# First dense attention: eviction of projections and turned sums on ACT, rotary products on POOL

## The chip, the cores and the metric

One core of one Trainium2 chip. The metric is the device time of the whole program in microseconds (us); lower is better. The program is a chain of eight layers' parts; the change touches only the first dense attention.

## The reference, cut to what matters

```python
def _L0_attn_ref(x, qkv_w, qkv_b, out_w, out_b):      # x: 4 x 1024 x 128, 16 heads of 8
    qkv = x @ qkv_w + qkv_b
    q, k, v = jnp.split(qkv, 3, axis=-1)
    ...
    q = apply_rotary(q)      # x1*cos - x2*sin, x2*cos + x1*sin
    k = apply_rotary(k)
    scores = jnp.einsum('bhqd,bhkd->bhqk', q, k) * SCALE
    weights = jax.nn.softmax(scores, axis=-1)
    attn = jnp.einsum('bhqk,bhkd->bhqd', weights, v)
    return attn.transpose(0, 2, 1, 3).reshape(B, T, D) @ out_w + out_b
```

## The kernel before, in words

The attention handles 4 batches of 8 pairs of heads, 32 pairs `p` in all, and each pair has 8 steps `k` of 128 keys. One generator, `order()`, writes down the work; every engine walks through the same list and picks its own items, so each engine's queue is in that order.

A step: PE makes four score blocks (L460, 128x512, three PSUM banks in turn: 4, 5 and 7), between them four blocks of scores for the row maxima of pair p+2 (L452, banks 0 to 3), and then the weighted sums of the step before (L534). ACT takes the exponential of each score block (L585), which frees its bank. DVE takes two row maxima (L640). Once in a pair come `parts` (four small DVE operations, L703 to L709, at step 0), `send` (step 1: a PE transpose, a DVE copy L716, and on SP a store L860 and, when it has landed, two loads L867, which bring the maxima to the operands of a later pair; a pair's first score waits for them) and `divide` (step 3).

`spread()` puts the preparation of the next batch into pairs 1 to 3 of each of the first three batches, always behind a step: eight `qk` items, a projection of 512 columns each (PE L468, two instructions), for query and key, for either half `hf`, and for x = 0 (the weights) and x = 1 (the weights with the columns of a turn swapped). They stand at steps 2, 5 and 7. Their PSUM bank is one of the three of the scores. DVE evicts them (L668): (product + bias) times cosine or sine, into `QF` and `R1`. After each x = 1 comes a `split` on POOL: the sum QF + R1 (L797), then four operations (L802 to L805) that split it into three bfloat16 parts, and SP stores these (L836). `QF` and `R1` are one set, so a `qk` waits until the `split` before has ended. The last `split` of a batch comes at step 5 of pair 3 of the batch (p = 3, 11, 19).

`fetch` (SP, L854, 24 DMAs of 64 KB) loads the operands of the next four pairs from these stores. For the next batch it stands at step 0 of pairs 4, 12 and 20, and waits for the stores of the last `split`. SP's queue is in order: the `send` of the following pair (its L860 and L867) stands behind it. The same holds of the `send` at step 1 of pair 3, which stands behind the stores of the third `split`.

POOL also gathers and adds the rows of the mixture of experts in pairs 1 to 9 (`row` items, L1131, L1140, L1143, four in a pair), in the same in-order queue as the splits.

At pairs 8, 16 and 24, steps 4 to 7, stand `turn` and `proj` of the batch before, twice each: a transposition of the attention's output on PE (L550), its eviction by DVE (L750), the output projection on PE (L557), and on DVE the addition to the residual (L759) and four statistics (L884). Those of the last batch end the stage.

Of the kernel before, what the change touches and what calls it, by code (L numbers as in the profile page):

```python
# [15 lines left out]
NB = 4  # L16
# [128 lines left out]
def program(nc, a, out):  # L145
    ctx = ExitStack()
    with ctx:
# [22 lines left out]
        def bank(key):  # L170
            return core.banks.of[key]
# [104 lines left out]
        def attention(first, wq, wk, wv, bq, bk, bvb, wo, extra, load, row, mix=None):  # L276
# [4 lines left out]
            with ExitStack() as c:  # L281
# [9 lines left out]
                part = [[sb([128, 512], BF16, c) for _ in range(3)] for _ in range(2)]  # L291
                QF = sb([128, 512], F32, c)
                R1 = sb([128, 512], F32, c)
                P = [sb([128, 4 if first else 8, 512], F32, c) for _ in range(4)]
                OS = sb([128, 512], F32, c)
                ATT = sb([128, 8, 128], F32, c)
# [143 lines left out]
                def pe(e):  # L440
# [22 lines left out]
                    for what, *i in order():  # L463
                        if what == "qk":
                            b, qi, hf, x = i
                            bm = early.next() if b == 0 else ring.next()
                            take(e, bm, (what, *i), (DV, (what, *i)))
                            e.op.matmul(PS[:, bm, :], W[qi][x], XT[:, b * T + hf * 512:b * T + hf * 512 + 512],  # L468
                                        start=True, stop=True).then_inc(*PM.up((what, *i)))
                        elif what == "v":  # L470
# [30 lines left out]
                        elif what == "tile":  # L501
                            p, ps, blk, ti = i
                            u0, nu = TILES[ti]
                            bk = 3 * (n % 2)
                            n += 1
                            if fills(p, 4 * ps + blk, ti):
                                bm = take(e, ring.next(), ("fill", *i))
                                e.op.matmul(PS[:, bm, 0:384], ident[:], XT[:, 0:384], start=True, stop=True)  # L508
                            take(e, bk, (what, *i), (AC if ps else PW, (what, *i)))
                            rows_in(e, p)  # L510
                            if gated(p, ps):
                                e.wait_ge(ONES, "ones")
                            for x in range(nu):
                                y = u0 + x
                                t = score(bk + x, p, 2 * blk + y // 4, y % 2, y // 2 % 2,
                                          KG if gated(p, ps) else KS)
                            t.then_inc(*SC.up((what, *i)))
                            SC.at["unit", p // 4] = SC.n
                        elif what == "pv":
                            p, kb = i  # L520
                            e.wait_ge(DV, ("v", p // 8, 1))
                            e.wait_ge(DV, "zeroed")
                            if first:
                                e.wait_ge(PW, (p, kb, 1, 1))
                            else:
                                e.wait_ge(DG, (p, kb // 2, 1 + kb % 2))
                            if kb == 0:
                                take(e, PVB, ("pv", p), (AC if first else DV, ("os", p)))
                            for side in range(2):
                                for hf in range(2):  # L530
                                    gq = 32 * (2 * side + hf)
                                    x = 2 * hf + side
                                    src = P[(8 * p + kb) % 4][:, x, :] if first else P[kb // 2][:, 4 * (kb % 2) + x, :]
                                    t = e.op.matmul(PS[gq:gq + 9, PVB, :], Vx[p // 8 % 2][:, kb, 8 * side + p % 8, :],  # L534
                                                    src, start=kb == 0, stop=kb == 7)
                            t.then_inc(*PV.up((p, kb)))
                        elif what == "divide":
                            p, = i
                            bm = take(e, ring.next(), ("divide", p), (DV, ("att", p)))
                            e.wait_ge(AC if first else DV, ("os", p))  # L540
                            for k in range(4):
                                t = e.op.transpose(PS[:, bm, k * 128:(k + 1) * 128], OS[:, k * 128:(k + 1) * 128],  # L542
                                                   ident[:])
                            t.then_inc(*PM.up(("divide", p)))
                        elif what == "turn":
                            b, j = i
                            bm = take(e, (ends if b == NB - 1 else ring).next(), ("turn", b, j), (DV, ("turn", b, j)))
                            e.wait_ge(DV, ("att", 8 * b + 7))
                            for k in range(4):
                                t = e.op.transpose(PS[:, bm, k * 128:(k + 1) * 128], ATT[:, 4 * j + k, :], ident[:])  # L550
                            t.then_inc(*PM.up(("turn", b, j)))
                        elif what == "proj":
                            b, j = i
                            bm = take(e, (ends if b == NB - 1 else ring).next(), ("proj", b, j), (DV, ("proj", b, j)))
                            e.wait_ge(DV, ("turn", b, j))
                            for k in range(4):
                                t = e.op.matmul(PS[:, bm, k * 128:(k + 1) * 128], ATT_T[j][:, 128 * k:128 * k + 128],  # L557
                                                wo, start=True, stop=True)
                            t.then_inc(*PM.up(("proj", b, j)))

                def act(e):
                    n = 0
                    loaded(e)
                    for what, *i in order():
# [9 lines left out]
                            e.op.copy(first_parts[qi][hf][1][:], QS[hf][:]).then_inc(*AC.up(("middle", qi, hf)))  # L574
                        elif what == "fetch" and i[0] == 0:
                            fetch_first(e, 1)
                        elif what == "step":
                            p, k = i
                            x = 8 * p + k
# [34 lines left out]
                def dve(e):  # L614
# [28 lines left out]
                    for what, *i in order():  # L643
                        if what == "qk":
                            b, qi, hf, x = i
                            bb = BB[qi][x]
                            e.wait_ge(PM, (what, *i))
                            if b == 0:
                                if qi:
                                    e.wait_ge(PO, ("split", 0, 0, hf))  # L650
                                src = PS[:, bank((what, *i)), :]
# [8 lines left out]
                                else:  # L660
# [1 line left out]
                                        *DV.up((what, *i)))  # L662
                                    DV.at["sum", qi, hf] = DV.n
                                continue
                            e.wait_ge(PO, ("split", b, qi, hf - 1) if hf else
                                      ("split", b, 0, 1) if qi else ("split", b - 1, 1, 1))
                            if first:
                                e.op.scalar_tensor_tensor(  # L668
                                    out=(QF, R1)[x][:], in0=PS[:, bank((what, *i)), :], scalar=bb,
                                    in1=extra[x][:, hf * 512:hf * 512 + 512], op0=ALU.add, op1=ALU.mult).then_inc(  # L670
                                    *DV.up((what, *i)))
                            else:
                                e.op.tensor_scalar(QF[:], PS[:, bank((what, *i)), :], bb, None, ALU.add).then_inc(  # L673
                                    *DV.up((what, *i)))
                        elif what == "split" and i[0] == 0:
# [54 lines left out]
                        elif what == "divide":  # L730
# [7 lines left out]
                            for side in range(2):  # L738
# [3 lines left out]
                                    view[:, side, :, :, 0:8],  # L742
                                    rc[:, side].unsqueeze(3).broadcast_to([128, 2, 4, 8]), ALU.mult).then_inc(
                                    *DV.up(("att", p)))
                        elif what == "turn":
                            b, j = i
                            e.wait_ge(PM, ("turn", b, j))
                            if b:
# [15 lines left out]
                def pool(e):  # L764
# [11 lines left out]
                    for what, *i in order():  # L776
# [9 lines left out]
                        elif what == "split":  # L786
                            b, qi, hf = i
                            pt = part[hf]
                            if b == 0:
                                e.wait_ge(AC, ("middle", qi, hf))  # L790
                                pt = first_parts[qi][hf]
                                e.op.tensor_tensor(pt[2][:], QS[hf][:], pt[1][:], ALU.subtract).then_inc(
                                    *PO.up(("split", b, qi, hf)))
                                continue
                            e.wait_ge(DV, ("qk", b, qi, hf, NX - 1))
                            if first:
                                then().tensor_tensor(QF[:], QF[:], R1[:], ALU.add).then_inc(*PO.up())  # L797
                            if qi:
                                e.wait_ge(SENT[hf], (b, 0, hf))
                            else:  # L800
                                e.wait_ge(SENT[hf], (b - 1, 1, hf))
                            then().tensor_copy(pt[0][:], QF[:]).then_inc(*PO.up())  # L802
                            then().tensor_tensor(QF[:], QF[:], pt[0][:], ALU.subtract).then_inc(*PO.up())
                            then().tensor_copy(pt[1][:], QF[:]).then_inc(*PO.up())
                            then().tensor_tensor(pt[2][:], QF[:], pt[1][:], ALU.subtract).then_inc(  # L805
                                *PO.up(("split", b, qi, hf)))

                def sp(e):
# [2323 lines left out]
```

## Time and profile before

| | |
|---|---|
| median of 3 runs | 4427.58 us (4419.74 to 4429.66) |
| the profiled execution | 4435.13 us, span 4433.3 us |
| PE, DVE, ACT, POOL busy, of the span | 76%, 62%, 57%, 31% |
| L640, row maxima, DVE | x512, 601.0 us busy, 1216 ns each |
| L585, exponentials, ACT | x1024, 532.4 us busy, 603 ns each |
| L460, scores of both attentions, PE | x3072, 738.6 us busy |

Busy time is the time in which an engine executes; the engines work side by side, so the shares do not add up. The stage of the change lies between 489 and 1231 us of the span.

### The profile page before, as it was taken

The page shows a single profiled execution, that of the slowest core. Times are in us where ns is not written, and L with a number is a line of the kernel's source. Part 1 is how long each engine was busy: PE and PEld are TensorE (multiplying, and loading weights), DVE is VectorE, ACT ScalarE, POOL GpSimd, SP SyncE. Part 2 cuts the span into 40 slices and gives each one's busy share as a digit, 9 for nine tenths or more (in the row PEclk, how much of TensorE's full clock was granted, in tenths as well). Part 3 has the DMA queues.
Part 4 walks back from the last instruction along what each step waited for, and adds up shares of the span by engine and source line. Part 5 has one row for each costly group of instructions (what it writes and reads, how often), then busy time and mean ns, then how long its engine had stood idle before and what let it go on. Part 6 is the DMA issues. An engine that isn't in the chain of part 4 may idle for free. (4 is left out here: it accounts for less than half of the span.)

```text
span 4433.3 us, 53632 instructions
## 1 busy us (share of the span) xinstructions
PE 3348.3 (76%) x20118; PEld 1505.0 (34%) x20182; DVE 2764.3 (62%) x4523; ACT 2540.8 (57%) x4189; POOL 1356.0 (31%) x1221
## 2 busy tenths in 40 slices
PE   7597788889948888988887887889868697541126
PEld 4265122212211222222222565466544274211124
DVE  5123889989736556655655776477667121488886
ACT  2112477767858989999995776377533222212225
POOL 0401283010012010010001885388411403218880
PEclk9698799999979999999997999899889798775558
DMA  4002121210020010010100111011020021550000
GB/s 136 33 22 57 29 48 32 33 31 16 2 47 17 14 27 17 15 23 7 15 1 29 28 35 36 14 34 35 17 81 8 30 60 33 73 66 0 10 5 24
DMA packets 140025, 137.36 MB, mean 31 GB/s; under 512 B 42184, under 2 KB 104692, under 8 KB 139764
## 3 DMA queue, kind: packets, MB, share of 16 engines
q1 hardware_dynamic: 130612, 116.07, 12.4%
q0 software_dynamic: 8192, 16.79, 1.6%
q8 instruction: 159, 2.61, 0.2%
q10 hardware_dynamic: 960, 1.05, 0.1%
q14 instruction: 102, 0.84, 0.1%
HBM read 64.90 MB, written 33.82 MB: 22 GB/s over the span
## 5 line engine op out<-in xcount | busy, mean ns | idle before, releaser
L460 PE MATMUL PS<-t 50*128 50x512 bf16 (+2 forms) x3072 | 738.6, 397 | 203.4 <-ACT t L603 53.8
L585 ACT ACTIVATE t<-PS 128x512 f32<-128x512 f32 x1024 | 532.4, 603 | 239.3 <-PE PS L460 233.9
L722 DVE TENSOR_TENSOR t<-t 128x1536 f32<-128x1536 f32 (+1 forms) x384 | 583.5, 1587 | 131.3 <-ACT t L603 77.8
L640 DVE TENSOR_REDUCE t<-PS 128x1 f32<-128x1024 f32 x512 | 601.0, 1216 | 54.0 <-PE PS L452 50.0
L534 PE MATMUL PS<-t 128*9 128x512 f32 x4096 | 551.1, 611 | 9.9 <-DVE t L722 9.5
L605 ACT ACTIVATE t<-PS 128x1536 f32<-128x1536 f32 (+1 forms) x384 | 477.7, 1311 | 53.7 <-PE PS L460 38.4
L603 ACT ACTIVATE t<-PS 128x1536 f32<-128x1536 f32 (+1 forms) x384 | 476.9, 1311 | 35.9 <-PE PS L460 20.9
L460 PEld LDWEIGHTS PS<-t 50*128 50x128 bf16 (+2 forms) x3072 | 158.4, 94 | 985.6 <-ACT t L603 276.2
L452 PE MATMUL PS<-t 48*128 48x512 bf16 x1024 | 342.0, 404 | 46.8 <-DVE t L640 24.0
L1798 POOL TENSOR_TENSOR t<-t 128x512 f32<-128x512 f32 x128 | 159.8, 1270 | 589.5 <-DVE t L1473 476.0
L2613 PE MATMUL PS<-t 128*128 128x32 f32 x256 | 61.1, 403 | 344.7 <-ACT t L2659 280.9
L508 PE MATMUL PS<-t 128*128 128x384 f32 x544 | 268.9, 579 | 1.6 <-DVE t L673 1.6
L1122 POOL DMA_INDIRECT scr<-t x128 | 126.3, 987 | 270.6 <-DVE t L1115 232.2
L2677 ACT COPY t<-PS 128x640 f32<-128x640 f32 x64 | 44.3, 692 | 277.0 <-DVE PS L2779 272.4
L1131 POOL DMA_INDIRECT t<-scr,t x128 | 123.6, 966 | 254.7 <-DMA scr<-t 181.9
L802 POOL CAST t<-t 128x512 bf16<-128x512 f32 x24 | 24.8, 1034 | 575.8 <-DVE t L673 574.2
L734 DVE RECIPROCAL t<-PS 128x16 f32<-128x16 f32 x64 | 16.5, 258 | 279.8 <-PE PS L542 277.0
L1685 ACT ACTIVATE t<-PS,t 128x128 f32<-128x128 f32 x512 | 179.9, 381 | 2.3 <-DVE t L1759 1.9
L2613 PEld LDWEIGHTS PS<-t 128*128 128x128 f32 x256 | 56.9, 328 | 350.2 <-ACT t L2659 285.6
L2177 PE MATMUL PS<-t 128*128 128x512 f32 x256 | 131.7, 665 | 26.8 <-issue 21.1
L2693 POOL TENSOR_TENSOR t<-t 128x256 f32<-128x256 f32 x124 | 104.4, 842 | 148.6 <-ACT t L2677 141.3
L1214 PE MATMUL PS<-t 128*128 128x320 f32 x512 | 149.6, 452 | 0.0
(403 smaller groups left out, 6380.0 us busy)
## 6 DMA issues: line engine op xcount, KB each, us to landing
t<-scr SPq DMA_DIRECT2D x336, 64.0 KB
t<-t SPq DMA_DIRECT2D x128, 128.0 KB, 2.3
scr<-t SPq DMA_DIRECT2D x96, 128.0 KB
t<-t SPq DMA_DIRECT2D x16, 512.0 KB, 13.3
scr<-t SPq DMA_DIRECT2D x2, 2560.0 KB
t<-scr SPq DMA_DIRECT2D x16, 320.0 KB, 3.6
scr<-t SPq DMA_DIRECT2D x16, 320.0 KB, 2.6
t<-scr SPq DMA_DIRECT2D x48, 48.0 KB
```

What stands on the lines that cost most here:

```text
L452: t = e.op.matmul(PS[:, 2 * side + hf, :], Qx[p // 4 % 2][lo:lo + KP, j, qc * 128:qc * 128 + 128], Kx[p // 4 % 2][lo:lo + KP, j, hf * 512: ...
L460: return e.op.matmul(PS[:, bk, :], Kx[p // 4 % 2][lo:lo + rows, j, kb * 128:kb * 128 + 128], Qx[p // 4 % 2][lo:lo + rows, j, hf * 512:hf * ...
L508: e.op.matmul(PS[:, bm, 0:384], ident[:], XT[:, 0:384], start=True, stop=True)
L534: t = e.op.matmul(PS[gq:gq + 9, PVB, :], Vx[p // 8 % 2][:, kb, 8 * side + p % 8, :], src, start=kb == 0, stop=kb == 7)
L585: e.op.activation(P[x % 4][:, 2 * hf + side, :], PS[:, bank((what, p, k, side, hf)), :], ACT.Exp, scale=S8).then_inc(*PW.up((p, k, side, hf)))
L603: t = e.op.activation(dst, PS[:, bk:bk + nu, :], ACT.Sigmoid, scale=S8)
L605: t = e.op.activation(dst, PS[:, bk:bk + nu, :], ACT.Exp, scale=S8)
L640: e.op.tensor_reduce(MX[p % 2][:, side, qc:qc + 1], PS[:, 2 * side:2 * side + 2, :].rearrange("p a n -> p (a n)"), AX, ALU.max).then_inc(* ...
L722: e.op.tensor_tensor(o, o, SGM[(12 * p + 3 * blk + ti) % 3][:, 0:nu, :], ALU.mult).then_inc(*DG.up((p, blk, ti)))
L1214: t = e.op.matmul(PS[:, b + hf, 0:320], ws[x % slots][i][:, f * 128:(f + 1) * 128], XE[x % 2][:, 320 * hf:320 * hf + 320], start=True, sto ...
L1685: e.op.activation(PB[i][:, h, :], PS[:, SB + h % 2, 128 * (h // 2):128 * (h // 2) + 128], ACT.Exp, bias=mx[i][:, h:h + 1], accum_out=su[i] ...
L1798: e.op.tensor_tensor(sn[:, :, :, lo:lo + 32], x[:, :, :, 32 - lo:64 - lo], TS[:, n % 8, :, lo:lo + 32].unsqueeze(2).broadcast_to([128, 2, ...
```

## The change

The projections of batches 1 to 3 are evicted by ACT, with the bias added and no factor; POOL multiplies both halves by cosine and sine ahead of the sum. `QF` and `R1` have a second set, one for each half. The turned sums are evicted by ACT too. Batch 0 and the second attention keep DVE. The diff in its parts: tiles, PE, ACT, DVE, POOL.

```diff
+                if first:
+                    QFs, R1s = (QF, sb([128, 512], F32, c)), (R1, sb([128, 512], F32, c))
+                else:
+                    QFs, R1s = (QF, QF), (R1, R1)
...
-                            take(e, bm, (what, *i), (DV, (what, *i)))
+                            take(e, bm, (what, *i), (AC if first and b else DV, (what, *i)))
...
-                            e.wait_ge(DV, ("turn", b, j))
+                            e.wait_ge(AC if first else DV, ("turn", b, j))
...
+                        elif what == "qk" and i[0] and first:
+                            b, qi, hf, x = i
+                            e.wait_ge(PM, (what, *i))
+                            if x == 0:
+                                e.wait_ge(PO, ("split", b, 0, hf) if qi else ("split", b - 1, 1, hf))
+                            e.op.activation((QFs, R1s)[x][hf][:], PS[:, bank((what, *i)), :], ACT.Identity,
+                                            bias=BB[qi][x]).then_inc(*AC.up((what, *i)))
+                        elif what == "turn" and first:
+                            b, j = i
+                            e.wait_ge(PM, ("turn", b, j))
+                            if b:
+                                e.wait_ge(PM, ("proj", b - 1, j))
+                            e.op.copy(ATT_T[j][:], PS[:, bank((what, *i)), :]).then_inc(*AC.up(("turn", b, j)))
...
-                            if first:
-                                e.op.scalar_tensor_tensor(
-                                    out=(QF, R1)[x][:], in0=PS[:, bank((what, *i)), :], scalar=bb,
-                                    in1=extra[x][:, hf * 512:hf * 512 + 512], op0=ALU.add, op1=ALU.mult).then_inc(
-                                    *DV.up((what, *i)))
...
-                        elif what == "turn":
+                        elif what == "turn" and not first:
...
-                            e.wait_ge(DV, ("qk", b, qi, hf, NX - 1))
+                            e.wait_ge(AC if first else DV, ("qk", b, qi, hf, NX - 1))
                             if first:
-                                then().tensor_tensor(QF[:], QF[:], R1[:], ALU.add).then_inc(*PO.up())
+                                ns = slice(hf * 512, hf * 512 + 512)
+                                e.op.tensor_tensor(QFs[hf][:], QFs[hf][:], extra[0][:, ns], ALU.mult).then_inc(*PO.up())
+                                e.op.tensor_tensor(R1s[hf][:], R1s[hf][:], extra[1][:, ns], ALU.mult).then_inc(*PO.up())
+                                then().tensor_tensor(QFs[hf][:], QFs[hf][:], R1s[hf][:], ALU.add).then_inc(*PO.up())
```

## Rows read from the trace of the kernel before

**Rows 1.** Stretches, all engines: length, busy (count) of each, granted clock, DMA share, GB/s.
```profile
489.00:1231.00 742.00, 658.66 (x4368) 158.56 (x4367) 641.12 (x813) 548.02 (x1056) 182.17 (x246) 0.97 0.14 28
845.60:866.00 20.40, 19.15 (x137) 4.39 (x133) 19.90 (x25) 17.00 (x34) 0.00 (x0) 1.00 0.01 2
915.90:939.90 24.00, 21.93 (x142) 4.99 (x143) 21.92 (x27) 17.16 (x33) 5.01 (x6) 1.00 0.10 34
581.80:610.20 28.40, 19.43 (x137) 4.46 (x133) 21.01 (x25) 17.23 (x34) 24.75 (x35) 0.90 0.44 95
...
1206.00:1226.00 20.00, 16.04 (x104) 3.73 (x100) 0.61 (x3) 16.96 (x34) 0.00 (x0) 1.00 0.00 1
```
**Rows 2.** Order of time about one projection: start, length, engine, line; idle time and its releaser.
```profile
957.84 1.12 PE L468 MATMUL PS<-t 128*128 128x512 f32 x2
959.01 0.75 DVE L668 SCALAR_TENSOR_TENSOR t<-PS,t 128x512 f32<-128x512 f32 x1 [0.57 <-PE PS L468]
959.38 1.58 ACT L585 ACTIVATE t<-PS 128x512 f32<-128x512 f32 x3 [1.42 <-PE PS L460]
...
959.82 0.39 PE L460 MATMUL PS<-t 50*128 50x512 bf16 x1 [0.31 <-DVE t L668]
```
**Rows 3.** Order of time, PE: first scores of pairs 5, 13 and 21.
```profile
610.24 0.61 PE L460 MATMUL PS<-t 50*128 50x512 bf16 x1 [7.45 <-DMA t<-scr]
...
800.75 0.60 PE L460 MATMUL PS<-t 50*128 50x512 bf16 x1 [4.29 <-DMA t<-scr]
...
992.20 0.61 PE L460 MATMUL PS<-t 50*128 50x512 bf16 x1 [7.91 <-DMA t<-scr]
```
**Rows 4.** Order of time, SP's queue: fetches and the sends beside them.
```profile
567.29 0.44 SPq L860 DMA_DIRECT2D scr<-t  x1
...
588.82 8.92 SPq L854 DMA_DIRECT2D t<-scr  x24
597.79 0.32 SPq L860 DMA_DIRECT2D scr<-t  x1
608.55 0.53 SPq L867 DMA_DIRECT2D t<-scr  x2
...
779.60 8.21 SPq L854 DMA_DIRECT2D t<-scr  x24
...
967.76 8.21 SPq L854 DMA_DIRECT2D t<-scr  x24
```
**Rows 5.** Order of time, POOL: first and last split of batch 1, last of batch 3.
```profile
528.62 1.28 POOL L797 TENSOR_TENSOR t<-t 128x512 f32<-128x512 f32 x1 [96.50 <-DVE t L668]
...
580.31 1.27 POOL L797 TENSOR_TENSOR t<-t 128x512 f32<-128x512 f32 x1
...
584.32 1.15 POOL L805 TENSOR_TENSOR t<-t 128x512 bf16<-128x512 f32 x1
...
959.84 1.28 POOL L797 TENSOR_TENSOR t<-t 128x512 f32<-128x512 f32 x1 [13.84 <-DVE t L668]
...
963.85 1.15 POOL L805 TENSOR_TENSOR t<-t 128x512 bf16<-128x512 f32 x1
```
**Rows 6.** Groups of ACT instructions: count, busy us, mean ns, idle before.
```profile
L612 ACT COPY t<-PS 128x512 f32<-128x512 f32 x32 | 18.7, 585 | 5.7 <-PE PS L534 4.4
...
L2938 ACT ACTIVATE t<-PS,t 128x512 f32<-128x512 f32 x32 | 20.2, 682 | 29.9 <-PE PS L2915 29.9
...
L2942 ACT ACT_TABLE_LOAD x1 | 1.3, 1283 | 0.0
```
**Rows 7.** Order of time, DVE and PE: second turned sum of pair 24.
```profile
1078.89 0.68 DVE L750 COPY t<-PS 128x512 f32<-128x512 f32 x1
1079.63 0.39 PE L460 MATMUL PS<-t 50*128 50x512 bf16 x1 [1.13 <-DVE t L750]
```
**Rows 8.** Order of time, POOL and DVE, in a split.
```profile
942.90 1.16 POOL L803 TENSOR_TENSOR t<-t 128x512 f32<-128x512 f32 x1
943.02 1.07 DVE L703 TENSOR_SCALAR t<-t 128x16 f32<-128x16 f32 x1
```

More of the change, by code:

```diff
@@ L546, in pe @@
                             b, j = i
-                            bm = take(e, (ends if b == NB - 1 else ring).next(), ("turn", b, j), (DV, ("turn", b, j)))
+                            bm = take(e, (ends if b == NB - 1 else ring).next(), ("turn", b, j), (AC if first else DV, ("turn", b, j)))
                             e.wait_ge(DV, ("att", 8 * b + 7))
@@ L646, in dve @@
                             bb = BB[qi][x]
-                            e.wait_ge(PM, (what, *i))
                             if b == 0:
+                                e.wait_ge(PM, (what, *i))
                                 if qi:
@@ L664, in dve @@
                                 continue
-                            e.wait_ge(PO, ("split", b, qi, hf - 1) if hf else
-                                      ("split", b, 0, 1) if qi else ("split", b - 1, 1, 1))
-                            if first:
-                                e.op.scalar_tensor_tensor(
-                                    out=(QF, R1)[x][:], in0=PS[:, bank((what, *i)), :], scalar=bb,
-                                    in1=extra[x][:, hf * 512:hf * 512 + 512], op0=ALU.add, op1=ALU.mult).then_inc(
-                                    *DV.up((what, *i)))
-                            else:
+                            if not first:
+                                e.wait_ge(PO, ("split", b, qi, hf - 1) if hf else
+                                          ("split", b, 0, 1) if qi else ("split", b - 1, 1, 1))
+                                e.wait_ge(PM, (what, *i))
                                 e.op.tensor_scalar(QF[:], PS[:, bank((what, *i)), :], bb, None, ALU.add).then_inc(
@@ L801, in pool @@
                                 e.wait_ge(SENT[hf], (b - 1, 1, hf))
[L802 to L805, printed above, removed]
+                            then().tensor_copy(pt[0][:], QFs[hf][:]).then_inc(*PO.up())
+                            then().tensor_tensor(QFs[hf][:], QFs[hf][:], pt[0][:], ALU.subtract).then_inc(*PO.up())
+                            then().tensor_copy(pt[1][:], QFs[hf][:]).then_inc(*PO.up())
+                            then().tensor_tensor(pt[2][:], QFs[hf][:], pt[1][:], ALU.subtract).then_inc(
                                 *PO.up(("split", b, qi, hf)))
```

## The prediction

> **What bounds the kernel now.** Read first the stretches [rows 1]. The stage takes 742 us; PE is busy for 658.7 of them, DVE for 641.1, ACT for 548.0, POOL for 182.2. A pair without any preparation takes 20.4 us (DVE 19.9, PE 19.15), which looks like a bound by DVE. The last two pairs show that it is not one: DVE has 0.61 us of work in 20.0 us there, and the pair is only 0.4 us shorter. What sets the step is a loop between PE and ACT: a score block, its exponential, the bank given back to the fourth score block, the weighted sums behind it. DVE runs beside it with a few tenths to spare.
>
> A pair with three projections takes 24.0 us, 3.6 more. The order of time [rows 2] says who makes that: PE works on a projection from 957.84 and begins the next score block at 958.90, 1.06 us later, and 3 x 1.06 = 3.2 of the 3.6 us. DVE evicts it in 0.75 us from 959.01, idle for 0.57 us before it; PE's third score block then waits for this bank (0.31 us, until 959.82), but its fourth waits for an exponential anyway. So the 0.75 us of DVE lie beside the loop, not on it.
>
> The second thing to see is the three stalls [rows 3]. PE sits idle for 7.45, 4.29 and 7.91 us before the first score of pairs 5, 13 and 21, each time for a load from DRAM, and pair 4 takes 28.4 us at a granted clock of 0.90 [rows 1]. SP's queue [rows 4] shows what the load waited for. The 24 loads of the fetch go out from 588.82; the store of pair 5's maxima goes out behind them at 597.79, lands behind them too, so that its loads go out at 608.55; pair 5 starts at 610.24. From the first load of the fetch to that start are 21.42 us; for the other two it is 800.75 - 779.60 = 21.15 and 992.20 - 967.76 = 24.44. The fetch itself waits for the stores of the batch's last split, which ends on POOL at 584.32 + 1.15 = 585.47 [rows 5], 3.35 us before 588.82. The chain in pairs 4, 12 and 20 is thus: last split on POOL, stores, fetch, send, first score. Whatever makes the last split later makes the next pair later by as much, since PE waits at the end of the chain in all three.
>
> **The change part by part.**
>
> POOL. Each of the 12 splits of batches 1 to 3 gets two products of 128x512 f32 by f32. The trace has no such product here; the sum L797 is the same form with two inputs in SBUF, 1.27 us [rows 5]. With the step between two dependent ones I take 2.62 us for the two. Lower bound 2.31 (twice the 1.15 of L805), upper 2.9 (1.41, the distance from L797 to the operation behind it, twice). A split grows from 963.85 + 1.15 - 959.84 = 5.16 us to 7.8. The ACT eviction in front ends about 0.1 us before the DVE one did; neglected.
>
> In batches 2 and 3 POOL is idle when the last split's input arrives (13.84 us before 959.84 [rows 5]). The split ends 2.6 us later, less 0.1: **+2.5 us each for pairs 13 and 21, +5.0 in all**.
>
> In batch 1 POOL works without a pause from 528.62, the first split, until past the last: rows of experts lie between the splits, so all four splits' growth adds up in front of the chain. The last split ended at 585.47; it now ends at about 585.47 + 4 x 2.62 = 595.95. The fetch goes out at about 599.3 and pair 5 starts at 620.7: **+10.5 us**. Range of this term: 9.2 to 11.6 by the bounds above. This is the large term. POOL's later rows move along with the pairs; the residual needs the eighth row at pair 8 and gets it long before.
>
> Other waits for POOL. ACT now waits for a split before it evicts the keys' projection of the same half, with the exponentials queued behind. In batch 1 that is the first split, over at 528.6 + 7.8 = 536.4, and the second, over near 556; the projections stand in pairs 2 and 3, which at 24 us each before 581.8 [rows 1] puts them near 551 and 566: no wait. The send of pair 4 stands in SP's queue behind the third split's stores (567.29 [rows 4]). This split now ends 3 x 2.62 = 7.9 us later, the store goes out near 575.1, its loads land some 4 us behind it, and pair 4 starts at 581.8 [rows 1]: 2 to 3 us to spare. The next thing to be late, but not yet.
>
> ACT. 24 projections and 8 turned sums. For the form with bias there are 32 evictions elsewhere, 682 ns each; the copy takes 585 [rows 6]. In [rows 2] ACT is idle for 1.42 us before the exponential at 959.38, and the product is ready at about 959.0. The eviction fits in, but ends late: successive ACT instructions start about 0.1 us before the end of the one in front, so the exponential moves from 959.38 to about 959.6, and the loop takes over what it loses. Cost 0.2 us for each projection; bounds 0 and 0.68 (whole eviction on the path). Only the 16 of batches 2 and 3 count; those of batch 1 lie before the stall that POOL sets. **+3.2 us** (0 to 11).
>
> DVE. It loses 24 x 0.75 and 8 x 0.68 = 23.5 us of work. Off the path, this is worth nothing except where PE really waited. Places are the turned sums: at 1079.63 PE had waited 1.13 us for the copy L750, which had waited for the row maxima behind the statistics [rows 7]. ACT takes it at once, but the row maxima stay, so I give back half: 0.6, and 0.4 in the pair after it, three times over: **-3.0 us** (-6 to 0). In the rest of the 24 projections I give back **-0.4**, and at the end of the stage the copies lie on the path but cost nearly the same.
>
> A rule against the change: [rows 8] show L703, an operation on 128x16 numbers, take 1.07 us while POOL's L803 runs; its neighbours take 0.2. DVE is held as long as POOL streams. The GPSIMD Engine Reference of the Trainium skill (Key points) says that the engine shares its SBUF interfaces with VectorE, in contention with VectorE's instructions in a 2-port mode or with two SBUF inputs; the trace agrees with it. By that rule alone the 24 new products would hold more of DVE's small operations.
>
> What this is here, from rows: the operations exposed are the four of `parts`, once in a pair; the row maxima read PSUM and keep their 1.2 us. The third split of a batch covers them already (943.02), and the longer one does again. The last split now covers those of pairs 4, 12 and 20, where PE waits for the chain anyhow. I take 0, bounds -1 and +1.3 for each of the two batches that count.
>
> **Sum**: 10.5 + 5.0 + 3.2 - 3.0 - 0.4 = +15.3 us, say 15. For the profiled execution 4435.1 + 15 = 4450; it lay 7.6 us above the median of the runs, 4427.6, for which I forecast **4443 us**, slower by 0.34%.
>
> **The rivals.**
>
> (1) *The chain gives the delay back*, so that the time stays. The fetch takes 21 to 24 us for the same bytes, by what else the DMA engines carry. A later fetch in batch 1 might run beside fewer gathers, or the stall in pairs 12 and 20 absorbs a part because DVE's relief moves the split itself earlier. Against it: in the third case POOL gathered nothing, and it was the slowest. With 3 us less in each of the three chains: 15 - 9 = +6, 4434 us.
>
> (2) *DVE is the bound*, faster. The place is every step of the pairs with projections: DVE is busy for 21.9 of 24.0 us there [rows 1]. If its freed 0.75 us shortened each of the 24 steps, and the 6 evictions of turned sums theirs, that is up to -22 us; against +15.5 of POOL's delay it leaves -6, or 4421 us. It decides once the projections give more than 0.65 us each. Against it: DVE idle 0.57 us ahead of L668, and the last two pairs.
>
> (3) *ACT is on the path with its whole eviction*, slower still. ACT's queue is in order, and an exponential that is ready must wait for PE's projection when this comes late. 30 x 0.6 = 18 us in place of 3.2: 4458 us. Against it: 1.42 us of idleness at just this place.
>
> (4) *Tables*. If the eviction's function made ACT load its tables anew, 48 loads at 1.28 us would make +62 us. In another stage the same function with bias (L2938) alternates with another one, with a single load [rows 6].
>
> (5) *The products move nothing*: if pair 5 is not held by POOL's chain but by the fetch's own DMA time, only batches 2 and 3 matter: about +5, 4433 us. Covered by the case of no change.
>
> **How the numbers follow.** Forecast 0.62, rivals (1) and (5) together 0.21, (2) 0.07, (3) 0.09, (4) 0.01. A change of less than 0.2%, 8.9 us, cannot be told from none. The forecast's own range is 4435 to 4452 (the POOL terms -2 to +2, ACT 0 to +6, DVE and landing times 3 either way), a tenth of it below the bound of 4436.4. Slower by over 0.2%: 0.62 x 0.88 + 0.1 + a fifth of (1) = 0.68; the same 0.24; faster 0.08. The range that holds 8 in 10: 4429 to 4456.
>
> **What would show it.** Right: the last split of batch 1 ends near 596 and the fetch goes out near 599; PE's idleness before the first score of pairs 5, 13 and 21 grows to about 17, 7 and 10 us; pairs 9 to 11 and 17 to 19 take within half a microsecond of what they took; no table load beside the exponentials. Wrong: a first score of pair 5 before 616, which would take the large term away; pairs with projections at 22 us, which would be rival (2); a stall at pair 4, whose send has 2 to 3 us to spare, and which would add to the sum.

## The result, and the profile after

Over 20 runs each, on the same chips, the median went from 4426.35 to 4442.26 us; the ratio is 1.0037, with a 95% interval of [1.0026, 1.0048], or 12 to 21 us. Forecast were 4443 us and +0.34%. The profiled execution of the changed kernel took 4446.85 us (span 4445.0), 11.7 more than that of the old one.

The stage went from 736.2 us (489.05 to 1225.27, first score to last) to 749.2 (491.14 to 1240.35). The new kernel starts the stage 2.1 us later, so moments are compared below as distances from the first score. The stretches, with the columns of [rows 1]: the stage, a pair without preparation, one with three projections, and pair 4.

```profile
491.00:1241.00 750.00, 654.03 (x4347) 157.58 (x4346) 620.11 (x778) 562.90 (x1085) 212.08 (x270) 0.97 0.14 28
861.20:881.60 20.40, 19.16 (x137) 4.41 (x133) 19.91 (x25) 17.00 (x34) 0.00 (x0) 1.00 0.01 2
931.40:955.50 24.10, 21.85 (x140) 5.07 (x139) 19.99 (x24) 18.72 (x36) 9.70 (x10) 1.00 0.10 34
583.40:627.60 44.20, 19.10 (x138) 4.39 (x135) 20.86 (x25) 17.26 (x34) 38.56 (x55) 0.77 0.38 68
```

DVE has 2 us less to do in a pair with projections, and the pair is 0.1 us longer. Pair 4 went from 28.4 to 44.2 us. The rows of PE with its idle time before the first scores of pairs 5, 13 and 21, for [rows 3]:

```profile
627.60 0.60 PE L464 MATMUL PS<-t 50*128 50x512 bf16 x1 [23.16 <-DMA t<-scr]
...
816.31 0.60 PE L464 MATMUL PS<-t 50*128 50x512 bf16 x1 [4.10 <-DMA t<-scr]
...
1007.74 0.61 PE L464 MATMUL PS<-t 50*128 50x512 bf16 x1 [7.17 <-DMA t<-scr]
```

SP's queue (L852 stores of a split, L870 fetch, L876 and L883 send), for [rows 4]:

```profile
576.93 0.45 SPq L876 DMA_DIRECT2D scr<-t  x1
...
597.51 1.45 SPq L852 DMA_DIRECT2D scr<-t  x3
600.92 8.29 SPq L870 DMA_DIRECT2D t<-scr  x24
609.25 0.32 SPq L876 DMA_DIRECT2D scr<-t  x1
625.95 0.53 SPq L883 DMA_DIRECT2D t<-scr  x2
...
799.06 8.20 SPq L870 DMA_DIRECT2D t<-scr  x24
...
986.02 8.19 SPq L870 DMA_DIRECT2D t<-scr  x24
```

POOL's last split of batch 1, for [rows 5]:

```profile
589.73 1.27 POOL L811 TENSOR_TENSOR t<-t 128x512 f32<-128x512 f32 x1
590.97 1.27 POOL L812 TENSOR_TENSOR t<-t 128x512 f32<-128x512 f32 x1
592.31 1.28 POOL L813 TENSOR_TENSOR t<-t 128x512 f32<-128x512 f32 x1
...
596.32 1.16 POOL L821 TENSOR_TENSOR t<-t 128x512 bf16<-128x512 f32 x1
```

It takes 7.75 us from 589.73 to 597.48; the old one took 5.16. One projection (L472), its eviction by ACT (L586), the exponentials behind (L602) and the third score block, for [rows 2]:

```profile
973.59 1.13 PE L472 MATMUL PS<-t 128*128 128x512 f32 x2
...
974.75 0.69 ACT L586 ACTIVATE t<-PS,t 128x512 f32<-128x512 f32 x1 [1.04 <-PE PS L472]
...
975.34 2.05 ACT L602 ACTIVATE t<-PS 128x512 f32<-128x512 f32 x4
975.50 0.39 PE L464 MATMUL PS<-t 50*128 50x512 bf16 x1 [0.24 <-ACT t L586]
```

The stage in segments, each the difference of two rows (old, new): start to first fetch 588.82 - 489.05 = 99.8, 600.92 - 491.14 = 109.8, so +10.0; pair 5 to the second fetch 169.4, 171.5, +2.1; pair 13 to the third 167.0, 169.7, +2.7; pair 21 to the end 233.1, 232.6, -0.5. The three stretches from fetch to first score make 67.0 and 65.7, -1.4. Sum +13.0.

### The profile page after: what moved, and what is told of

Read it like the earlier page. It is cut to its first block and busy times, and to the rows that moved or that the text cites. A ratio compares the mean times of both kernels' runs of the same rounds, so it can differ in the third digit from the quotient of the medians.

```text
span 4445.0 us, 53700 instructions
## 1 busy us (share of the span) xinstructions
PE 3365.0 (76%) x20182; PEld 1511.2 (34%) x20182; DVE 2746.9 (62%) x4491; ACT 2557.4 (58%) x4221; POOL 1381.1 (31%) x1245
## 5 line engine op out<-in xcount | busy, mean ns | idle before, releaser
L464 PE MATMUL PS<-t 50*128 50x512 bf16 (+2 forms) x3072 | 747.9, 400 | 207.8 <-ACT t L622 46.6
L602 ACT ACTIVATE t<-PS 128x512 f32<-128x512 f32 x1024 | 531.4, 604 | 207.0 <-PE PS L464 203.5
L620 ACT ACTIVATE t<-PS 128x1536 f32<-128x1536 f32 (+1 forms) x384 | 476.8, 1311 | 39.3 <-PE PS L464 28.4
L456 PE MATMUL PS<-t 48*128 48x512 bf16 x1024 | 345.0, 404 | 46.3 <-DVE t L657 24.4
```

What stands on the lines that cost most here:

```text
L456: t = e.op.matmul(PS[:, 2 * side + hf, :], Qx[p // 4 % 2][lo:lo + KP, j, qc * 128:qc * 128 + 128], Kx[p // 4 % 2][lo:lo + KP, j, hf * 512: ...
L464: return e.op.matmul(PS[:, bk, :], Kx[p // 4 % 2][lo:lo + rows, j, kb * 128:kb * 128 + 128], Qx[p // 4 % 2][lo:lo + rows, j, hf * 512:hf * ...
L602: e.op.activation(P[x % 4][:, 2 * hf + side, :], PS[:, bank((what, p, k, side, hf)), :], ACT.Exp, scale=S8).then_inc(*PW.up((p, k, side, hf)))
L620: t = e.op.activation(dst, PS[:, bk:bk + nu, :], ACT.Sigmoid, scale=S8)
```

## The experiments

In all ratios the kernel before on the same chip is the base. Brackets are 95% intervals. Steps and stages are read from one profiled execution each.

**Without POOL's products.**

```diff
-  e.op.tensor_tensor(QFs[hf][:], QFs[hf][:], extra[0][:, ns], ALU.mult)...
-  e.op.tensor_tensor(R1s[hf][:], R1s[hf][:], extra[1][:, ns], ALU.mult)...
```

> The changed kernel without POOL's two products by cosine and sine in batches 1 to 3 (the turn of queries and keys is left out there; the sum and the parts stay). Theory, the split on POOL holds the chain to the fetch and the send: each split is 2.6 us shorter, the last one of batch 1 ends 10.5 us earlier (near 587), pair 5 starts that much earlier, pairs 13 and 21 by 2.5 us each; about 15.5 us less than the changed kernel, near 4427, level with the kernel before. Rival, ACT's evictions on the path of the exponentials make the loss: the time stays near 4442, since they all stay.

Ratio 1.0003 [0.9989, 1.0017], 15 us below the changed kernel's 1.0037. ACT's evictions are all there (24 steps behind projections still take 2.63 or 3.22 us), and the loss is gone; the two intervals do not overlap. The last split of batch 1 ended 97.5 us after the first score (590.03 - 492.55) in place of 106.3, and the first fetch went out after 102.1 us (594.62 - 492.55), 7.7 sooner than in the changed kernel, where 10.5 were expected:

```profile
584.86 1.27 POOL L811 TENSOR_TENSOR t<-t 128x512 f32<-128x512 f32 x1
...
588.87 1.16 POOL L819 TENSOR_TENSOR t<-t 128x512 bf16<-128x512 f32 x1
...
594.62 8.45 SPq L868 DMA_DIRECT2D t<-scr  x24
```

The profiled execution, at 4451.42 us the slowest of the 12, shows less than the ratio: its stage took 745.1 us, only 4.1 less than the changed kernel's. The way from the second fetch to pair 13 took 25.3 us there in place of 17.3, and the last pair took 3.9 us longer, with a granted clock of 0.82 from 1210 to 1238 us. So the size of the loss rests on the ratio, and its place on the earlier split and fetch. The loss is POOL's delay.

**Twice the products.**

```diff
+  e.op.tensor_tensor(EX[:], extra[0][:, ns], extra[1][:, ns], ALU.mult)...
+  then().tensor_tensor(EX[:], extra[0][:, ns], extra[1][:, ns], ALU.mult)...
```

> The changed kernel with two more products of the same form in each split (into a tile that nobody reads). Theory, the chain: each split grows by another 2.6 us, the last of batch 1 ends 10.5 us later (near 608), pairs 13 and 21 start 2.6 us later each; about 15.5 us more than the changed kernel, 1.0035 of it, near 1.007 of the old one. The send of pair 4, with 2 to 3 us to spare, is now late: PE stands idle some 3 to 5 us before pair 4, which pair 5's stall absorbs. Rival, a fetch that starts later lands faster: the first delays are given back, less than 8 us more.

Ratio 1.0102 [1.0081, 1.0123], on a chip where the old kernel takes 4279.93 us: some 28 us more than the changed kernel's ratio gives there, not 15.5. The chain did what was expected: the first fetch 121.1 us after the first score (+11.3), a stall now before pair 4 as well, though 1.74 us and not 3 to 5. The rest is in pairs 9 to 11 and 17 to 19: from pair 5 to the second fetch +7.3 against the changed kernel, from pair 13 to the third +7.2, where 2.6 each were forecast. The order of time (POOL and DVE, in step 1 of pair 10) shows the start of it:

```profile
684.12 1.16 POOL L822 TENSOR_TENSOR t<-t 128x512 f32<-128x512 f32 x1
...
685.20 0.18 DVE L717 TENSOR_SCALAR t<-t 128x16 f32<-128x16 f32 x1
685.35 0.61 POOL L823 CAST t<-t 128x512 bf16<-128x512 f32 x1
685.41 0.58 DVE L721 CAST t<-t 128x16 bf16<-128x16 f32 x1
...
686.04 1.18 POOL L824 TENSOR_TENSOR t<-t 128x512 bf16<-128x512 f32 x1
...
686.11 1.14 DVE L723 TENSOR_TENSOR t<-t 128x16 f32<-128x16 f32 x1
```

The first split, 10.3 us long now (676.88 to 687.22), reaches the four operations of `parts` in the next pair. Two of the four are held until a POOL operation ends: L721 takes 0.58 us (to 685.99; L823 ends at 685.96) and L723 takes 1.14 (to 687.25; L824 ends at 687.22). The two that fell between POOL's operations took 0.18 and 0.17. Step 2 of that pair took 6.33 us in place of 3.43. Not all of it is the hold: PE waited, and then ran at a granted clock of 0.50, the lower of the two levels, from 690.1 to 693.5. Pair 18, held in the same way, kept 1.00 and took 4.73. Step 2 of the two pairs:

```profile
687.60:693.90 6.30, 5.12 (x19) 0.94 (x18) 4.37 (x5) 2.28 (x4) 1.69 (x4) 0.73 0.21 68
887.40:892.10 4.70, 3.53 (x19) 0.73 (x18) 4.38 (x5) 2.28 (x4) 0.00 (x0) 1.00 0.26 87
```

So the hold cost 1.3 us there and the lower clock behind it 1.6. Pairs 11 and 19, where a longer third split covers the same operations, grew by 3.5 us each. Beyond the chain's 2.6 us, each of two batches lost 4.6 to 4.7 more, and these pairs are where: they grew by 6.5 us in batch 2 and by 4.8 in batch 3. The contention, which I had priced at 0, cost next to nothing more while a split took 7.7 us, and at 10.3 us, with the lower clock behind it, more than the chain in these two batches.

**The send ahead of the fetch**, in the old and in the changed kernel, each run twice (e2 and e3 on one chip, e9 and e10 on another).

```diff
-  if p % 4 == 0 and k == 0 ...: yield "fetch", p // 4 + 1
   ...
   if k == 1 and 2 <= p + 1 < NP: yield "send", p + 1
+  if p % 4 == 0 and k == 1 ...: yield "fetch", p // 4 + 1
```

> The kernel before with one thing moved: the fetch stands behind the send at step 1 of its pair, not at step 0 in front of it. Theory: the idle times of PE before the first scores of pairs 5, 13 and 21 (7.45, 4.29, 7.91 us) go to under 1 us, and with them the slow first step behind each (3.7 in place of 2.4 us); 24 us less than the kernel before, near 4402. Rival, the transfers themselves set it: the send of the pair after lands behind the fetch instead, the idle time moves to pairs 6, 14 and 22, and the time stays within 5 us of before.

> The same move of the fetch in the changed kernel. Theory: POOL's longer splits now end in a gap that nobody waits for, so the two kernels meet: 4402 to 4406, within 4 us of the old kernel with the same move (3.2 us of ACT's delay against 3.4 us of DVE's relief); each projection still makes its next step 0.2 us longer. Rival, the loss lies in POOL's and ACT's work itself and not in the chain: it stays some 16 us slower than the old kernel with the move, near 4418.

> The old kernel with the send first once more, to stand on one chip beside the next three. Ratio to the old kernel 0.995 to 0.996. Theory, POOL holds the maxima's small operations: step 2 of pairs 11 and 19 is 4.7 us or more, longer where TensorE falls to half clock in it.

> The changed kernel with the send first, on the same chip. Theory, without the chain the two kernels differ by the steps alone: 0 to 4 us below the old one in the same order, ratio 0.9945 to 0.9955. Rival, a real gain by DVE's relief: 7 us below, as the first pair of ratios had it (0.9946 against 0.9962).

Old 0.9962 [0.9948, 0.9975] and 0.9965 [0.9953, 0.9978]; changed 0.9946 [0.9928, 0.9964] and 0.9966 [0.9950, 0.9983]. The second pair of runs has them equal (medians 4413.44 and 4413.13 us). The 0.0016 between the first two (4417.34 and 4407.62 us) did not come back, and 0.9966 lies outside the 0.9945 to 0.9955 that was expected. Stages in the second pair of runs: old 713.3, changed 712.1 us (the stretches of the two, whole stage):

```profile
491.20:1204.50 713.30, 649.81 (x4343) 157.56 (x4346) 639.50 (x808) 546.93 (x1054) 182.72 (x246) 0.99 0.15 29
```
```profile
490.90:1203.00 712.10, 648.44 (x4343) 157.65 (x4346) 620.11 (x778) 562.62 (x1084) 212.48 (x270) 1.00 0.15 29
```

In the old one PE is never idle before a pair's first score. In the changed one it is once, for 0.61 us before pair 6: the first fetch goes out only 2.7 us before pair 5 starts, and the store of pair 6's maxima stands behind it and takes 15.4 us (610.45 to 625.87). The rival was right to that extent. SP's queue of the old one, first run (L862, L869 send; L856 fetch):

```profile
593.12 0.32 SPq L862 DMA_DIRECT2D scr<-t  x1
594.48 0.54 SPq L869 DMA_DIRECT2D t<-scr  x2
595.13 8.21 SPq L856 DMA_DIRECT2D t<-scr  x24
614.11 0.32 SPq L862 DMA_DIRECT2D scr<-t  x1
616.93 0.53 SPq L869 DMA_DIRECT2D t<-scr  x2
```

The store lands in 1.36 us ahead of the fetch; behind it, it had taken 10.8. The gain was expected at 24 us and is 15 to 17 by the ratios, while the stages of the two profiles were 20 and 23 us shorter than in the old profile. That one was itself 8.8 us slower than the old kernel's median (4435.13 against 4426.35), so stages and medians need not agree; where the rest of the gain went in other executions stays open. With the chain out of the way, the change is worth nothing that the runs can tell: 19.4 us less work on DVE, 16 more on ACT, 30 more on POOL, 1.2 us of stage.

**Rows of experts moved out of the pairs with splits**, in the changed kernel.

```diff
-  if mix and p and k % 2 == 0 and 4 * (p - 1) + k // 2 < NC + 4:
+  if mix and p % 8 > 3 and k % 2 == 0 and 4 * (p - 4 - 4 * (p // 8)) + k // 2 < NC + 4:
```

> The changed kernel with the rows of experts in pairs 4 to 7 of each batch, none in the pairs with splits. Theory, the rows between the splits of batch 1 add up their growth: the last split of batch 1 starts as soon as its projection is there and ends about 10.5 us earlier (near 587), pair 5 starts 10.5 us earlier, near 4432 in all; pairs 13 and 21 stay as they are. Rival, the landing time of the fetch is what grew (26.7 us against 21.4 in the profile): pair 5 does not move, 4442.

Ratio 1.002 [1.0002, 1.0038], 4435.13 us; this interval reaches the changed kernel's 1.0037, so the time alone settles nothing, and the reading rests on the profile. Its stage took 740.2 us, 9.0 less than the changed kernel's. The last split of batch 1 found POOL idle and ended at 584.97:

```profile
577.21 1.28 POOL L811 TENSOR_TENSOR t<-t 128x512 f32<-128x512 f32 x1 [11.32 <-ACT t L586]
...
583.82 1.15 POOL L821 TENSOR_TENSOR t<-t 128x512 bf16<-128x512 f32 x1
```

The fetch went out 100.75 us after the first score, 9.0 sooner than in the changed kernel; pair 5 started 12.8 sooner, the rest being landing time. The queue of rows was what added up. Within pair 4, PE, DVE and ACT then stood still for 3.9 to 5.5 us while POOL went on; the last section shows it. Before pair 5 PE was then idle for only 0.55 us, still for the load, so the standstill made that first score no later.

**The turned sums alone on ACT**, old kernel with the send first: the lines of the diff for `turn`, those for `qk` left out.

> The old kernel with the send first and with the turned sums alone evicted by ACT, for the sizes of steps. Theory, DVE's relief: step 7 of pairs 8, 16 and 24 from 4.60 to 4.00 us, step 5 from 3.52 to 3.63, so 1.5 us in all; steps behind projections stay at 2.43. Rival, ACT's place costs as much as DVE's: no step moves by more than 0.1 us.

> The old kernel with the send first and the turned sums alone on ACT, timed. The steps of its profile give 1.5 us less than the old one with the send first: ratio 0.9945 to 0.9955, not to be told from the changed kernel with the send first. Rival, the projections on ACT bring a gain of their own: then this one lies 4 us above that.

Step 7 of pairs 8, 16 and 24: 4.00 us in place of 4.60 (of 6.22 in one case, where the granted clock fell); step 5: 3.63 in place of 3.52; steps behind projections 2.43, as before. Ratio 0.9955 [0.9939, 0.9971], 4408.76 us: 4.7 us below the old kernel with the send first and 4.4 below the changed one on the same chip, both inside the intervals. The stage is 712.1 us, the changed kernel's to 0.1 us. So the steps show DVE's relief at the turned sums, 1.5 us in all, which the time of the program is too coarse to confirm, and the projections on ACT add nothing to it.

**Projections at steps 2, 3 and 4**: the old kernel with the send first, the changed one, and the old one with the second set of buffers alone (DVE evicts into `QFs[hf]`, `R1s[hf]` and waits as ACT does in the change).

```diff
+  ks = (2, 3, 4) if first else (2, 5, 7)
-  if b + 1 < NB and i in (1, 2, 3) and k in (2, 5, 7):
+  if b + 1 < NB and i in (1, 2, 3) and k in ks:
```

> The old kernel with the send first and with the projections at steps 2, 3 and 4 of pairs 1 to 3, in place of 2, 5 and 7. The third split of a batch then ends before the maxima's small DVE operations of the next pair. Theory, POOL holds these DVE operations: the long step 2 of pairs 3, 11 and 19 (6.18, 6.35 and 6.36 us, with TensorE at half clock in it) falls to 3.7, about 8 us less than with the send first alone, near 0.9944 of the old kernel. Rival, the step is long for the DVE eviction of its projection: it stays above 4.7, and the crowded steps 3 and 4 cost 1 to 2 us more.

> The changed kernel with the send first and the projections at steps 2, 3 and 4. Theory: as for the old one, step 2 of pairs 11 and 19 falls from 4.51 to 3.4, 2 us less in all, near 0.994 of the old kernel, level with the old kernel in the same order within 3 us. Rival, DVE's relief is worth more where projections stand close together: 5 us below the old one in this order.

> The old kernel with the send first, the projections at steps 2, 3 and 4, evicted by DVE with their factors as before, but with the second set of buffers. Theory, the single set made DVE wait for POOL there (PE idle 2.9 and 2.5 us in each batch): these waits go, the stage loses some 16 us against the kernel with one set (729.6 us), and it comes within 4 us of the changed kernel in this order (709.3). Rival, DVE has no room for evictions in steps that follow each other: 5 to 10 us of the 20 stay.

One set: ratio 0.9992 [0.9981, 1.0004], a stage of 729.6 us; 0.9944 was expected, and it is slower than the send first alone. Step 2 of pairs 11 and 19 fell to 3.59, as expected of the held operations, but DVE now waits for POOL to clear the buffers, and PE for DVE, for 2.9 and 2.5 us in each batch (rows of the first projection that waits, in batch 2):

```profile
653.59 0.75 DVE L671 SCALAR_TENSOR_TENSOR t<-PS,t 128x512 f32<-128x512 f32 x1 [3.08 <-POOL t L808]
...
654.40 0.60 PE L463 MATMUL PS<-t 50*128 50x512 bf16 x1 [2.91 <-DVE t L671]
```

Changed kernel, on the same chip: 0.9959 [0.9947, 0.9971], stage 709.3. It was expected level with the old one in this order and is 14.7 us below it, since it has the second set. Step 2 of pairs 11 and 19 fell from 4.51 to 3.59 (forecast 3.4). Two sets and DVE: 0.9955 [0.9938, 0.9973], 4405.95 us, stage 707.3, within 4 us of 709.3 as expected. It is the shortest stage of all, 6 us under the old kernel with the send first on the same chip, and the lowest of the four medians there (base 4428.41), though its ratio cannot be told from those of the other kernels with the send first, the one-set kernel aside. The second set is what this order needs; ACT and POOL are not.

## Why the prediction was right, by its steps

*POOL, batch 1, +10.5.* Measured 10.0 to the fetch: four splits, grown by 2.59 each, with POOL never idle between them. *Batches 2 and 3, +5.0.* A split of the last batch takes 7.74 us (975.52 to 983.26) against 5.16. With everything in them, the segments grew by 2.1 and 2.7 us, less than 2.5 + 1.6 of ACT each. In batch 3 DVE gave some back. In batch 2 the sum had no term for what did most: pair 11 got 1.4 us shorter, since its step 2 took 6.37 us in the old profile, with a projection of 2.08 us (1.12 elsewhere) at a granted clock of 0.53, and 4.52 in the new one. The sign that pairs 9 to 11 and 17 to 19 keep their length within half a microsecond failed there and for pair 17, which grew by 0.7.

*ACT, 0.2 a projection.* The step behind a projection went from 2.43 to 2.63 us (at step 3 from 3.02 to 3.22) for 21 of the 24; for the other three, behind step 7 of pairs 1, 9 and 17, it had been 2.60 before. The eviction took 687 ns (forecast 682). No table load appeared.

*DVE, -3.0 and -0.4.* Too much. Step 7 of pairs 8, 16 and 24 gave the 0.6 us (0.9 in pair 16), but step 5 took 0.11 back; with all their steps the three pairs gave 2.2. The 0.4 expected in the pair after did not come: its step 1 stayed at 3.72 us in pairs 9 and 25 and went from 3.38 to 3.72 in pair 17, since statistics and residual sum stay on DVE. Step 2 of pairs 10 and 18 gave 0.25 each. About -2.3 in all, where -3.4 was forecast.

*Contention, 0.* Right as a difference, for this change: the third split held L721 for 1.13 us where it had held L703 for 1.07 [rows 8], and step 2 of pair 19 went from 4.74 to 4.53. The hold costs about 1.1 us in either kernel (step 2 of pair 18 takes 3.68 and 3.43). In pair 3 it went away (step 2 from 4.74 to 3.43 us), and in pairs 12 and 20, where PE waits for the chain anyhow, step 2 went from 2.54 to 2.87. At 10.3 us a split reached further ones.

```profile
959.02 1.30 POOL L813 TENSOR_TENSOR t<-t 128x512 f32<-128x512 f32 x1
959.22 1.13 DVE L721 CAST t<-t 128x16 f32<-128x16 bf16 x1
```

*The chain passes the delay on.* Yes, but with a spread I had only as a rival: from fetch to first score 21.4, 21.1, 24.4 us in the old profile, 26.7, 17.3, 21.7 in the new. My forecast of PE's idle times (17, 7, 10) met 23.2, 4.1 and 7.2. Each of the three is off by 3 to 6 us, and that their sum, 34, came out right is luck. So is part of the hit on the total: the stage grew by 13.0 us and the median by 15.9, and the interval of 12 to 21 us would have held other sums too. What the experiments bear out is the mechanism, the delay of the last split passed on by the fetch.

## What to carry to other kernels

Work that is moved to an idle engine is free only if nobody waits for that engine's results: a share of 31% busy said nothing here, since four splits in an in-order queue stood in front of a fetch. Look for the transfer that stands behind another in a queue without needing it; moving one line there was worth 0.35%, while the move of the evictions, with the chain out of the way, was worth nothing that the runs can tell. And ask of a freed engine whether it was the bound: the last pairs, with almost no work on DVE and 3 us less on PE, were only 0.4 us shorter, so there was little to win.

## What the runs showed of the hardware

The same 24 transfers of 64 KB delayed the store behind them very differently: from fetch to first score it took 17.3 to 26.7 us in the profiles of the old and the changed kernel, and 21.2, 21.2 and 21.3 in the one with twice the products, on a chip where the old kernel took 4280 us. In that profile POOL gathered rows beside the first fetch and not beside the other two, so the gathers did not set it there; what makes the spread stays open.

DVE's operations on 128x16 numbers in SBUF, 0.17 to 0.18 us alone, ended 0.03 us after the POOL operation on 128x512 beside them where one held them (1.07, 1.13, 0.58 and 1.14 us in the rows above).

In the profile of the moved rows, PE stood for 5.5 us, ACT for 5.3 and DVE for 3.9 in the middle of pair 4, beside a fetch and POOL's gathers. The trace names PE's wait as one for DVE and the other two as ended by something remote, so it does not show the cause:

```profile
599.62 0.26 DVE L747 RECIPROCAL t<-PS 128x16 f32<-128x16 f32 x1 [3.85 <-remote]
...
599.71 0.60 ACT L602 ACTIVATE t<-PS 128x512 f32<-128x512 f32 x1 [5.29 <-remote]
```

A standstill of the same kind stands in the profile with two sets and DVE, in pair 2, beside gathers again: ACT idle for 2.6 us and DVE for 2.2, so that step 0 took 5.75 us in place of 2.43.
